# A linear-attention stage on one core: GpSimd adds the row's negative cumulative sum, ScalarE takes one exponential of 512 columns in place of four of 128

## What is computed

```
cla   = cumsum(log(alpha + 1e-6))              # per chunk and head, over its 128 tokens
decay = exp(cla - swapaxes(cla, -1, -2))       # 128 x 128 per chunk and head
decay = where(causal, decay, 0)
attn  = (q @ k^T) * beta^T * decay
y_local = attn @ v
kw    = k * beta * exp(cla_end - cla)
state = state * exp(cla_end) + v^T @ kw
y     = y_local + (q @ state) * exp(cla)
```

## Time and profile before

| | us |
|---|---|
| median of 3 runs | 959.72 (959.37 to 959.97) |
| the profiled execution | 959.89 |
| its span, first to last instruction | 958.2 |
| stage A and the first weights of the mid stage | about 20 to 244 |

### The profile page before, as it was taken

The page is one execution under the profiler, slowest core; times in us unless marked ns, Lnnn a source line. Parts: engine busy times, 40 slices in busy tenths (PEclk is TensorE's granted clock), DMA queues, the critical chain, the costliest instruction groups (busy, mean ns, idle before and its releaser), DMA issues.

```text
span 958.2 us, 13269 instructions
## 1 busy us (share of the span) xinstructions
PE 940.9 (98%) x4725; PEld 534.3 (56%) x4744; DVE 609.0 (64%) x1128; ACT 460.3 (48%) x918; POOL 479.3 (50%) x487
## 2 busy tenths in 40 slices
PE   6999999999999999999999999999999999999998
PEld 4888888888734454444544455445454444544443
DVE  7455656849677576776865466445475676766543
ACT  4443324356577545664433355323454665456630
POOL 5433424377366676666840043304233466665575
PEclk9999999999999999999999999999999999999999
DMA  9401300024210000000000000000000000110001
GB/s 319 167 12 34 132 23 23 1 89 133 89 43 0 1 1 1 1 1 1 1 1 1 1 1 1 1 1 1 1 1 1 1 0 1 45 44 1 1 23 67
DMA packets 14738, 30.31 MB, mean 32 GB/s; under 512 B 2064, under 2 KB 2128, under 8 KB 14672
## 3 DMA queue, kind: packets, MB, share of 16 engines
q1 hardware_dynamic: 14672, 29.45, 8.8%
HBM read 25.22 MB, written 4.23 MB: 31 GB/s over the span
## 4 chain that ended last, share of the span: by engine, by line
PE 91%; DVE 3%; ACT 2%; POOL 1%; issue 1%; DMA 1%; SPq 0%; POOLq 0%; DVEq 0%
PE psum L2066 53%; PE psum L2280 14%; PE psum L2282 13%; PE psum L2408 7%; PE psum L2097 2%; PE psum L2419 1%; DMA wqk_raw<-wk 1%; PE psum L2175 1%; DVE wv_lo L1507 1%; PE psum L2086 1%; ACT probs L1324 0%; DVE xb_lo L1974 0%; ACT xb_hi L1330 0%; POOL hid L865 0%; DVE smax L1966 0%
## 5 line engine op out<-in xcount | busy, mean ns | idle before, releaser
L869 POOL TENSOR_TENSOR hid<-hid,hid_hi 128x512 f32<-128x512 f32 x88 | 102.7, 1167 | 96.5 <-DVE hid_hi L1767 96.5
L2280 PE MATMUL psum<-xf,w_gu 128*128 128x512 f16 x352 | 133.8, 380 | 0.0
L2280 PE MATMUL psum<-xf,w_s 128*128 128x512 f16 x264 | 100.1, 379 | 1.1 <-DVE up L1740 0.5
L2282 PE MATMUL psum<-xf,w_gu 128*128 128x512 f16 x264 | 100.1, 379 | 0.0
L1188 ACT ACTIVATE hid_lo<-hid 128x512 f16<-128x512 f32 x88 | 55.0, 625 | 40.2 <-POOL hid L869 40.2
L865 POOL TENSOR_TENSOR hid<-up,gate 128x512 f32<-128x512 f32 x44 | 56.1, 1274 | 21.7 <-ACT gate L1183 21.7
L2282 PE MATMUL psum<-xq,w_s 128*128 128x512 f16 x176 | 66.7, 379 | 0.0
L2280 PEld LDWEIGHTS psum<-xf,w_gu 128*128 128x128 f16 x352 | 34.3, 97 | 54.1 <-ACT acc L1173 15.5
L1183 ACT ACTIVATE gate<-gate,sg_xs 128x512 f32<-128x512 f32 x44 | 31.7, 721 | 58.7 <-DVE gate L1750 58.6
L731 POOL TENSOR_TENSOR xrstd<-xvar,minus_half 128x1 f32<-128x1 f32 x48 | 25.9, 549 | 65.3 <-DVE xvar L1443 65.3
L1767 DVE TENSOR_SCALAR hid_hi<-hid 128x512 f16<-128x512 f32 x88 | 39.1, 445 | 26.7 <-POOL hid L865 25.1
(11 more groups left out here) (307 smaller groups left out, 2553.2 us busy)
## 6 DMA issues: line engine op xcount, KB each, us to landing
cla_wide<-cla_dram SPq DMA_DIRECT2D x16, 256.0 KB, 3.3
out<-xres SPq DMA_DIRECT2D x16, 256.0 KB, 2.0
xres<-x SPq DMA_DIRECT2D x3, 1024.0 KB, 13.2
codes_gu<-gateT SPq DMA_DIRECT2D x1, 2816.0 KB, 11.5
codes_gu<-upT SPq DMA_DIRECT2D x1, 2816.0 KB, 10.9
codes_da<-downT SPq DMA_DIRECT2D x1, 1536.0 KB, 6.8
codes_db<-downT SPq DMA_DIRECT2D x1, 1280.0 KB, 9.9
xres<-x SPq DMA_DIRECT2D x4, 256.0 KB, 3.4
```

The costliest lines, as they stand in the source:

```text
L869: nc.gpsimd.tensor_tensor(hid[:, :], hid[:, :], hid_part(hid_hi, j, half), ALU.subtract).then_inc(rest_done, 1)
L2280: nc.tensor.matmul(bank(use[0]), w, x_operand(piece, k, False), start=start and k == 0, stop=False, skip_group_check=not start)
L2282: last = nc.tensor.matmul(bank(use[0]), w, x_operand(piece, k, True), start=False, stop=k == 1, skip_group_check=not start)
```

## The change

GpSimd gets a second instruction behind the mask, in place on the same buffer: it adds `cla_minus` (four columns of the chunk, each broadcast over its head's 128 columns). Since it reads what the mask has written, it waits for it by a new semaphore `cla_step`, and it takes over ScalarE's wait for `cla_minus`. ScalarE then makes one exponential of 512 columns without a bias.

```
                     nc.gpsimd.affine_select(out=wide, in_=wide, compare_op=ALU.is_ge, fill=MASKED, base=0,
                                             pattern=[[0, HEADS], [1, P]], channel_multiplier=-1
-                                            ).then_inc(cla_masked, 1)
+                                            ).then_inc(cla_step, 1)
+                    pool.wait_ge(cla_step, n + 1)
+                    pool.wait_ge(cla_minus_done, 2 * b + s + 1)
+                    i = 16 * s + 4 * c
+                    nc.gpsimd.tensor_tensor(wide, wide, cla_minus[:, i:i + 4].unsqueeze(2).broadcast_to([P, HEADS, P]),
+                                            ALU.add).then_inc(cla_masked, 1)
...
-                    act.wait_ge(cla_minus_done, 2 * b + s + 1)
                     act.wait_ge(cla_masked, b * 8 + (n + 1))
-                    for h in range(HEADS):
-                        i = 16 * s + 4 * c + h
-                        last = nc.scalar.activation(cols(decay, h, P), cols(cla_wide[n % 2], h, P), ACT.Exp,
-                                                    bias=cla_minus[:, i:i + 1])
-                    last.then_inc(decay_done, 1)
+                    nc.scalar.activation(decay[:, :], cla_wide[n % 2][:, :], ACT.Exp).then_inc(decay_done, 1)
```

More of the change, by code:

```diff
@@ L315, in hybrid_layer_kernel @@
     cla_masked = sem("cla_masked")
+    cla_step = sem("cla_step")
     cla_minus_done = sem("cla_minus_done")
```

## The result

| | median, us | lowest to highest | executions |
|---|---|---|---|
| before | 959.89 | 959.23 to 960.75 | 13 |
| changed | 962.17 | 961.47 to 962.72 | 13 |

The ratio is 1.0022, with a 95% interval of 1.0015 to 1.0029, which is 1.4 to 2.8 us. The profiled execution has a span of 960.6 us against 958.2 before. TensorE's granted clock is full in both (its mean is 1.000, and 0.999 before).

What follows compares the result with a forecast made beforehand. PE, busy 940.9 of 958.2 us, bounds the kernel; all costs 0 except 2.1 us at the end of stage A: span 958.2 + 2.1 = 960.3, median from 959.72 to 961.8, range 959.9 to 963.0.

Steps and rivals of the forecast that it cites:

- The prices: Per chunk: the add on POOL 1.04 us, one 512-column exponential 0.62; ACT gets back about 10 us in all.
- First batch and (1, 0): First batch: cost 0, POOL has waits to fill; second batch's chunk (1, 0): `decay` 0.5 us later, covered.
- (1, 1): Second batch: the two L1449 end 0.6 us later, first L1639 1.15 later, POOL's scaling L808 0.9 late.
- (1, 2): Second batch: `kw` ends at 224.3, not 222.08; L808 comes at 227.6; PE's transposes 0.2 us late, covered.
- (1, 3): Second batch's last chunk: POOL and DVE take turns, the fourth low part ends at 237.6, PE 2.4 us late.
- The walk: Trace rows of POOL and DVE moved forward with the add; 1.7 to 3.0 us lost as prices vary.
- The cover: Before PE's scores at 230.00: PE stood 0.94 us for the state, which hides late transposes.
- the edge: L808 of 226.77: from a delay of 0.85 us on, each further tenth goes to PE.
- clearly slower: Rival: POOL bounds the X chunks, late keys of (1, 3) use up the state's cover; 3 to 4.5 us, chance 0.06.
- a wait for `kT` at 230: Sign: if PE waits there for `kT` or the state, POOL's backlog was larger than thought.
- the last term: Collision of POOL's X step with DVE's four low parts at the end of stage A: 2.1 us.
- The test at the end: Sign before the mid stage: PE waits about 2 us for `qk_lo`; the four take 5 to 6 us, not 2.85.

## Why the prediction was right, point by point

- **What bounds the kernel.** PE, and ScalarE's relief worth nothing: shown by the run without the add (960.21 for 960.02, and PE's waits from 30 to 260 us unchanged).
- **The prices.** Add 1.04 us, foreseen 1.04. Exponential 0.63, foreseen 0.62. ACT's busy time fell by 9.4, foreseen 10.
- **First batch and (1, 0).** Cost 0, as the run with the first 13 chunks shows. `attnT` of (1, 0) started at 202.77, foreseen 202.8.
- **(1, 1).** The two `xn` took 2.25 us, foreseen 2.3:

```profile
206.75 2.25 DVE L1450 TENSOR_SCALAR xn<-xres,xmv,xrstd 128x512 f32<-128x512 f32 x2
206.80 1.04 POOL L823 TENSOR_TENSOR cla_wide<-cla_wide,cla_minus 128x512 f32<-128x512 f32 x1
207.80 0.93 POOL L741 TENSOR_TENSOR x_last<-x_mid,x_first 128x256 f32<-128x256 f32 x1
```

- **(1, 2).** `kw` was to end at 224.3 and ended at 224.29; the scaling of `kn` was to come at 227.6 and came at 227.61; PE's transposes were to be 0.2 late and were 0.24 late (228.70 for 228.46):

```profile
222.79 1.50 POOL L831 TENSOR_TENSOR kw<-kn,decay 128x512 f32<-128x512 f32 x1
...
227.61 1.04 POOL L809 TENSOR_TENSOR kn<-kn,kscale 128x512 f32<-128x512 f32 x1
```

- **(1, 3).** The walk had the add end at 230.35, the fourth low part at 237.6 and PE's product with k = 3 at 237.68. It was 230.37, 237.65 and 237.70.
- **The cover was used up.** I wrote that the late keys are covered by the state's wait of 0.94 us and that the walk stands at the edge. PE started the scores at 230.04 in place of 230.00, and what came last was `kT`, with 0.69 us:

```profile
230.04 1.16 PE L2067 MATMUL psum<-qT,kT 128*128 128x128 f32 x8 [0.69 <-ACT kT L1094]
```

The delay of `kn` is 0.84 us against the 0.85 that I gave as the edge. In the changed kernel's profile a first bit went to PE already, as the rival "clearly slower" has it: from `state,qT` of (1, 2) (225.77 now, 225.78 before) to that of (1, 3) PE takes 5.27 us in place of 5.18. These 0.09 us lie ahead of the leg and come on top of its 2.30. It is one profile: in the other kernels with the last adds the same stretch has 5.18 or 5.19. I had named a wait for `kT` at 230 as the sign that POOL's backlog was larger than I think; it came, and the backlog was the one that I walked. The sign was badly chosen, since at the edge either of the two can come last. The named wait for `attnT` (0.16 us) was not foreseen; it costs 0.06.

- **The sum.** 961.8 was forecast, 962.17 measured, inside 959.9 to 963.0. Of the 0.37 us between them, 0.17 are the base: the kernel before has 959.89 at the median of 13 executions, and I counted from the 959.72 of three. The other 0.2 are the last term: the walk itself gave 2.4 us, and I took 2.1, the middle of the walks with other prices. Measured were 2.30 by the leg and 2.28 by the medians. The prices had their rows, so the walk deserved more trust than its neighbours. That it came out to 0.1 us, instruction by instruction, is more than its own spread of 1.7 to 3.0 us promised, and in part luck. The test at the end, "a PE wait of about 2 us in total and 5 to 6 us for the four", came out as 1.7 and 5.52. The 1.7 is less than the 2.39 that these three steps lost, for two reasons that the rows of PE show. The products overlap (one takes 0.39 us, and the next starts 0.23 behind it), so 0.16 us of each delay is not counted as idle: 0.32 + 0.61 + 0.73 + 3 x 0.16 = 2.14. And the first product behind a wait takes 0.50, and its successor comes 0.34 behind it in place of 0.23: 0.11 for k = 2 and for k = 3, together 2.36.

## What to carry to other kernels

Before work goes to an engine with idle time, look at what its next instructions collide with when they come later, not at its busy share: here 13 of 16 equal instructions cost nothing, and the last three pushed a queue into the one place where the engine that sets the end had 0.5 us of room. In this kernel GpSimd's time and VectorE's were one budget wherever VectorE read two SBUF inputs, so walk both lists together, turn by turn, and price a shift in whole turns. One input from PSUM, or the other engine's work moved by a few instructions, removed the collision here, and the leg of the trace between two products of the bounding engine shows it more finely than the time of the execution.

## What the runs showed of the hardware

- Four exponentials of 128 columns take 1.27 us with a column as bias and 0.91 without (median of one 0.392 and 0.298): of ScalarE's saving of 0.64 us per chunk, 0.36 came from the bias that is gone and only 0.28 from making one of four. The Trainium skill has this price, in "ScalarE: Activation LUTs", section "What ACT_TABLE_LOAD costs": about 93 ns for each pointer operand, and 93 ns of overlap between neighbours. The trace agrees: 0.094 us for the bias, and about as much of overlap in a row of four, (4 x 0.298 - 0.91) / 3. I had overlooked it.
- The exclusion is by whole instructions and in turns, and it lengthens both sides: the X low part on POOL took 1.67 in place of 1.16, the weights' low part on DVE 1.65 in place of 0.68. Over the kernel DVE's busy time grew by 4.2 us with an unchanged list. Here a longer duration of an unchanged instruction was thus a sign of the neighbour, not of more work.
